# One rotary product per projection with its exchanged half from a VectorE shuffle, and new places for all operations of the layers and the closing block

## The chip, the core and the metric

The kernel runs on one core of one Trainium2 chip. The core has five engines that follow their own instruction lists: PE (TensorE, with its weight loads PEld), DVE (VectorE), ACT (ScalarE), POOL (GpSimd) and SP (SyncE, which issues the DMAs). They meet through semaphores alone. The metric is device time in microseconds (us), lower is better: the kernel before takes 2342.19 us, the median of three runs.

## The reference, cut to what matters

Four sequences of 512 rows of 128 channels go through a slot attention, a mixture of experts, six transformer layers and a quantised feed-forward block. The six layers are what the change touches:

```python
def _rope(x):                      # HD = 8, half = 4
    x1, x2 = (x[..., :half], x[..., half:])
    return concatenate([x1 * cos - x2 * sin, x1 * sin + x2 * cos], axis=-1)

for i in range(NL):                # NL = 6 layers, 16 heads of 8 channels
    xn = _adaln(x, noise_emb, n1_w[i], n1_b[i])
    q, k, v = split(xn @ qkv_w[i].T, 3)
    a = _attn(_rope(q), _rope(k), v, src_mask) @ so_w[i].T;  x = x + a
    xn = _adaln(x, noise_emb, n2_w[i], n2_b[i])
    q = _rope(xn @ cq_w[i].T);  k = _rope(context @ ck_w[i].T)
    a = _attn(q, k, context @ cv_w[i].T, ctx_mask) @ co_w[i].T;  x = x + a
    xn = _adaln(x, noise_emb, n3_w[i], n3_b[i])
    x = x + (gelu(xn @ f1_w[i].T + f1_b[i]) @ f2_w[i].T + f2_b[i])
```

## The kernel before, in words

Six layers times four sequences are 24 *visits*, `VISITS`. The four visits of a layer are independent of each other, and visit v needs the result of visit v - 4. The kernel runs them as a software pipeline that is written out by hand. Three tables of numbers, `OFFSETS`, `LAYER_OFFSETS` and `BLOCK_PLACES`, give every operation a place, with a step of `PERIOD` from visit to visit. `Places.moments` sorts the places of one engine, and each engine runs its operations in that sorted order. The numbers are nothing but sort keys: what an operation waits for is set by its semaphores, and an engine never runs ahead of an operation that waits.

One visit is this chain. `normalise_rows` (POOL) makes normal rows, `turn_rows` (PE, L1398) transposes them, `scale_shift` (ACT, L1598) applies the gain. `product` (PE, L1406) multiplies by the query and the key weights and, in the rotary step, by a second copy of each whose rows are exchanged by halves of a head (`qr`, `kr`, later `cqr`): so the two halves of a pair of PSUM banks hold the product and its exchanged product. `turn_products` (DVE, L1842) multiplies both by cosine and sine in one operation of 1024 columns, `rotate` (POOL, L1744) adds the halves. Then the sum is split into three bf16 parts: `first_part` (ACT, L1609), `less_first` (POOL, L1748), `second_part` (ACT, L1613), `third_part` (POOL, L1754). SP stores the parts to DRAM and loads them back in another layout (`store_queries`, `store_stage`, `load_queries`, `load_keys`).

The self attention of a visit takes 32 *max* steps (PE L1281 scores, DVE L1826 row maxima), in four groups, each followed by a split of the maxima (POOL L1757 to L1760), a transposition (PE L1348), a copy (ACT L1575) and two small DMAs. Then come 32 *exp* steps (PE L1292 shifted scores, ACT L1561 exponentials) and 16 products with the values (PE L1328). L1365 and L1372 transpose sums and rows, L1381 projects and L1871 (DVE) adds to the state. Cross attention is the same with L1315/L1833 (max), L1303/L1561 (exp) and L1340. The feed-forward part is L1438, L1634 and L1447. The `context` keys get the same rotary treatment once a layer, in two halves (L1414, L1849).

All scores, the rotary products and the feed-forward products take turns in a ring of three pairs of PSUM banks (`shared(..., 3)`): a PE step waits until the reader of the step that used its pair last is done. One further bank, `aux`, serves transpositions and projections one at a time. POOL and SP run their own lists in order, so a step that waits there holds all that stand behind it.

The closing block (four passes, b = 0 to 3, one per sequence; its DVE work at L1907 to L2013) starts for a sequence when the last layer's visit of that sequence is done, and so runs beside the visits 20 to 23.

Of the kernel before, what the change touches and what calls it, by code (L numbers as in the profile page):

```python
# [56 lines left out]
SECTION_GROUPS = {"next": ("n1", "q", "qr", "k", "kr", "v"), "self": ("so", "n2", "cq", "cqr"), "context": ("ck", "ckr", "cv"),  # L57
# [731 lines left out]
def store_key_part(sp, dst, parts, stage, stored):  # L789
# [5 lines left out]
VISITS = LAYERS * B  # L795
PER_UNIT = 2 * TB
# [4 lines left out]
N_HALF = B // 2 * N_CTX  # L801
# [5 lines left out]
PERIOD = 7152  # L807
OFFSETS = {
    "PE exp": (
        -54, 274, 479, 1118, 1587, 1668, 2002, 2177, 2281, 2529, 2558, 2737, 2915, 3047, 3271, 3428, 3673, 3908, 4042, 4177, 5174, 5350,  # L810
        5514, 5712, 5842, 5899, 6019, 6151, 6222, 6342, 6516, 6678),
    "ACT exp": (
        0, 328, 559, 1192, 1648, 1752, 2045, 2219, 2335, 2575, 2679, 2783, 3015, 3119, 3314, 3497, 3716, 3954, 4097, 4231, 5217, 5404,
        5568, 5755, 5896, 6000, 6104, 6208, 6312, 6416, 6558, 6720),
    "PE max": (
        -4071, -3915, -3695, -3574, -3537, -3301, -3267, -2938, -2712, -2313, -1955, -1933, -1769, -1604, -1474, -1276, -967, -20, 308,
        513, 677, 939, 1084, 1275, 1430, 1624, 1801, 1968, 2126, 2317, 2495, 2703),
    "DVE max": (
# [3 lines left out]
    "POOL split": (-2758, -1083, 1507, 3051),  # L822
    "PE turn maxima": (-2338, -201, 3104, 3394),
    "ACT copy maxima": (-1998, -123, 3217, 3439),
    "SP rows": (-1920, -45, 3295, 3517),
    "ACT copy": (4449, 6971),
    "PE gather": (4574, 7378),
    "DVE divide": (4642, 7446),
    "PE turn on": (7583,),
    "ACT copy on": (7651,),  # L830
    "PE project": (7921,),
    "DVE add": (8048,),
    "PE cross turn on": (16742,),
    "ACT cross copy on": (16820,),
    "PE cross project": (16900,),
    "DVE cross add": (17027,),
    "PE cross exp": (14938, 15050, 15181, 15221, 15457, 15615, 15811, 16139),
    "ACT cross exp": (15022, 15126, 15235, 15339, 15595, 15751, 15855, 16215),
    "PE cross max": (13529, 13642, 13691, 13803, 13868, 13950, 13990, 14128),
    "DVE cross max": (13564, 13688, 13768, 13850, 13930, 14010, 14090, 14170),  # L840
    "PE cross pv": (15291, 15479, 16007, 16333),
    "POOL cross split": (14270,),
    "PE cross turn maxima": (14407,),
    "ACT cross copy maxima": (14452,),
    "SP cross rows": (14530,),
    "ACT cross copy": (15693, 16450),
    "PE cross gather": (15834, 16528),
    "DVE cross divide": (15912, 16606),
    "DVE moments cross": (8407,),
    "DVE seed cross": (9124,),  # L850
    "POOL norm cross": (9212,),
    "PE turn cross": (10009,),
    "ACT scale cross": (10087,),
    "DVE moments ff": (17103,),
    "DVE seed ff": (17335,),
    "POOL norm ff": (17460,),
    "PE turn ff": (18000,),
    "ACT scale ff": (18118,),
    "DVE moments next": (-8255,),
    "DVE seed next": (-8135,),  # L860
    "POOL norm next": (-8047,),
# [145 lines left out]
def layers(nc, a, m, sem):  # L1007
# [88 lines left out]
    with nc.Block() as block:  # L1096
# [156 lines left out]
        def _(pe):  # L1253
# [147 lines left out]
            def product(kind, half, i):  # L1401
# [5 lines left out]
                if half:  # L1407
                    got.then_inc(x_ps[kind], 1)
# [888 lines left out]
```

## Time and profile before

| what | value |
|---|---|
| median of three runs | 2342.19 us (2342.07 to 2351.33) |
| the profiled execution | 2346.46 us |
| its span, first to last instruction | 2344.7 us |
| granted TensorE clock, mean | 0.904 |
| PE busy / weight loads busy | 1883.7 us (80%) / 798.6 us (34%) |
| DVE busy | 1655.5 us (71%) |
| ACT busy | 1483.1 us (63%) |
| POOL busy | 929.8 us (40%) |

A busy PE is the union of its matmuls' spans, whose ends are modelled and which overlap. The layers begin at about 424 us. From about 650 us to 1990 us every visit looks like the one before it; ahead of that the pipeline fills, and behind it the visits run out while the closing block runs.

### The profile page before, as it was taken

To read this page: it belongs to the slowest core of one execution; us is meant where nothing else is said; L and a number is where in the kernel's file an instruction comes from. 1 tells how busy PE (TensorE), PEld (TensorE's weight loads), DVE (VectorE), ACT (ScalarE), POOL (GpSimd) and SP (SyncE) were. 2 spreads that over 40 slices of the span, in tenths; PEclk is the share of its full clock that TensorE was granted. 3 is DMA by queue.
4 is the path that set the end of the run, shared out by engine and by line. 5 is a ranking of instruction groups with operands and counts; after the bars stand their busy time and mean duration, and the time that the engine had idled before them with its cause. 6 is when DMAs were issued, how large, how long until landed. Compare 5 with 4: busy or idle time off the path is not lost.

```text
span 2344.7 us, 36580 instructions
## 1 busy us (share of the span) xinstructions
PE 1883.7 (80%) x13318; PEld 798.6 (34%) x13318; DVE 1655.5 (71%) x3027; ACT 1483.1 (63%) x1840; POOL 929.8 (40%) x1420
## 2 busy tenths in 40 slices
PE   3564381167899999999999999999999999988651
PEld 2333271012233333333333333333334333333321
DVE  7766011367788887888878887888888887786456
ACT  2442020035678878878887877888877887767442
POOL 2443705123244453444444344444444445423421
PEclk9776696579999999999999999999999999989765
DMA  2001121322233433323433324432432333411100
GB/s 95 1 1 42 49 96 47 85 55 63 59 71 83 92 81 89 76 55 82 105 86 70 83 64 88 91 83 69 97 80 60 76 93 87 90 38 37 33 6 9
DMA packets 153713, 156.45 MB, mean 67 GB/s; under 512 B 32247, under 2 KB 137523, under 8 KB 153523
## 3 DMA queue, kind: packets, MB, share of 16 engines
q1 hardware_dynamic: 151487, 149.91, 27.1%
q0 software_dynamic: 2048, 4.20, 0.6%
q8 instruction: 107, 1.75, 0.3%
q14 instruction: 71, 0.58, 0.1%
HBM read 83.73 MB, written 67.85 MB: 65 GB/s over the span
## 4 chain that ended last, share of the span: by engine, by line
PE 58%; DVE 14%; ACT 4%; issue 4%; POOL 1%; DMA 1%; SPq 0%; POOLq 0%; DVEq 0%; ACTq 0%
PE ps L1328 14%; PE ps L1292 7%; DVE smax L1826 6%; PE ps L1281 6%; PE ps L1406 6%; PE ps L1447 4%; PE ps L1438 4%; PE ps L1340 4%; ACT big L1561 2%; PE ps L1381 2%; DVE rot L1842 2%; PE ps L1365 2%; PE ps L1303 1%; PE ps L1315 1%; PE ps L1398 1%
## 5 line engine op out<-in xcount | busy, mean ns | idle before, releaser
L1561 ACT ACTIVATE big<-ps 128x1024 f32<-128x1024 f32 x960 | 956.2, 1027 | 258.8 <-PE ps L1292 240.2
L1826 DVE TENSOR_REDUCE smax<-ps 128x2 f32<-128x1024 f32 x768 | 921.7, 1221 | 261.5 <-PE ps L1281 255.7
L1328 PE MATMUL ps<-big,vaug 128*32 128x512 f32 x3072 | 412.1, 615 | 2.9 <-ACT big L1561 2.9
L1281 PE MATMUL ps<-k,q 49*128 49x512 bf16 x1536 | 294.1, 391 | 64.3 <-DVE smax L1826 35.5
L1292 PE MATMUL ps<-q,k 52*128 52x512 bf16 x1536 | 295.4, 387 | 12.1 <-DVE smax L1826 5.6
L1757 POOL CAST mparts<-smax 128x16 bf16<-128x16 f32 x96 | 19.5, 203 | 569.1 <-DVE smax L1826 569.1
L1281 PEld LDWEIGHTS ps<-k,q 49*128 49x128 bf16 x1536 | 72.7, 94 | 310.5 <-DVE smax L1826 105.4
L1406 PE MATMUL ps<-xnT,w 128*128 128x512 f32 x288 | 166.8, 665 | 0.9 <-ACT xnT L1598 0.9
L1833 DVE TENSOR_REDUCE maxima<-ps 128x8 f32<-128x616 f32 x192 | 144.6, 795 | 31.6 <-PE ps L1315 30.0
L1292 PEld LDWEIGHTS ps<-q,k 52*128 52x128 bf16 x1536 | 75.2, 94 | 195.0 <-issue 90.2
L1748 POOL TENSOR_TENSOR hat<-rot,rparts 128x512 f32<-128x512 f32 x72 | 83.6, 1161 | 112.2 <-ACT rparts L1609 112.2
L1744 POOL TENSOR_TENSOR rot<-rot 128x512 f32<-128x512 f32 x72 | 91.5, 1271 | 74.2 <-DVE rot L1842 72.9
L1340 PE MATMUL ps<-big,vcaug 128*32 128x512 f32 x768 | 104.9, 617 | 14.3 <-ACT big L1561 6.5
L1754 POOL TENSOR_TENSOR rparts<-hat,rparts 128x512 bf16<-128x512 f32 x72 | 83.5, 1159 | 69.7 <-ACT rparts L1613 69.7
L1447 PE MATMUL ps<-w,hT 128*128 128x128 f32 x768 | 109.6, 287 | 1.6 <-ACT hT L1634 1.6
L1438 PE MATMUL ps<-xnT,w 128*128 128x512 f32 x192 | 108.6, 664 | 1.9 <-ACT xnT L1598 1.9
L1447 PEld LDWEIGHTS ps<-w,hT 128*128 128x128 f32 x768 | 92.5, 191 | 35.7 <-issue 32.5
L1842 DVE TENSOR_TENSOR rot<-ps,cs 128x1024 f32<-128x1024 f32 x72 | 87.7, 1218 | 22.8 <-PE ps L1406 21.9
L1328 PEld LDWEIGHTS ps<-big,vaug 128*32 128x32 f32 x3072 | 63.4, 109 | 116.1 <-issue 94.3
L1303 PE MATMUL ps<-cq,kc 52*128 52x512 bf16 x384 | 71.8, 394 | 11.4 <-DVE smax L1826 4.5
L1598 ACT ACTIVATE xnT<-ps,gain_next 128x512 f32<-128x512 f32 x24 | 18.5, 773 | 98.4 <-PE ps L1398 98.4
L311 PE MATMUL ps<-ident,hat 128*128 128x128 f32 x96 | 23.3, 389 | 68.0 <-DVE hat L126 48.1
(302 smaller groups left out, 2877.4 us busy)
## 6 DMA issues: line engine op xcount, KB each, us to landing
q<-scratch_queries SPq DMA_DIRECT2D x48, 384.0 KB, 5.6
k<-scratch_keys SPq DMA_DIRECT2D x48, 384.0 KB
cq<-scratch_cross_queries SPq DMA_DIRECT2D x48, 384.0 KB, 6.3
scratch_queries<-rparts SPq DMA_DIRECT2D x24, 384.0 KB, 2.4
scratch_keys<-rparts SPq DMA_DIRECT2D x24, 384.0 KB, 2.6
scratch_cross_queries<-rparts SPq DMA_DIRECT2D x24, 384.0 KB
scratch_queries<-rparts SPq DMA_DIRECT2D x24, 256.0 KB, 2.7
scratch_keys<-rparts SPq DMA_DIRECT2D x24, 256.0 KB, 2.8
```

What stands on the lines that cost most here:

```text
L1281: last = nc.tensor.matmul(out[:, u], m.q6[rows, v % 2, 2 * g + pr, qt * P:(qt + 1) * P], m.k6[rows, v % 2, 2 * g + pr, :], start=True, sto ...
L1292: last = nc.tensor.matmul(out[:, u], m.k6[rows, v % 2, 2 * g + pr, kt * P:(kt + 1) * P], m.q6[rows, v % 2, 2 * g + pr, :], start=True, sto ...
L1303: last = nc.tensor.matmul(out[:, u], m.kc6[rows, v % B, pair, :], m.cq[rows, pair, :], start=True, stop=True)
L1328: last = nc.tensor.matmul(m.ps[32 * j:32 * j + 32, pv_bank, :], of_head(m.vaug, v % 2 * TB + kt, g, j), of_quad("self", q)[:, j, :], start ...
L1340: last = nc.tensor.matmul(m.ps[32 * j:32 * j + 32, aux, :], of_head(m.vcaug, v % B, g, j), of_quad("cross", n)[:, j, :], start=(g % 2 == 0 ...
L1406: got = nc.tensor.matmul(banks(kind, i)[:, half, :], w_of(m, names[half]), m.xnT[:, xn[of_turn, i], :], start=True, stop=True)
L1438: nc.tensor.matmul(banks("up", 2 * v + c // 2)[:, c % 2], w_of(m, "f1")[:, c * P:(c + 1) * P], m.xnT[:, xn["ff", v], :], start=True, stop= ...
L1447: last = nc.tensor.matmul(m.ps[:, aux, t * P:(t + 1) * P], m.hT1[:, c, t * P:(t + 1) * P], w_of(m, "f2")[:, c * P:(c + 1) * P], start=(c = ...
L1561: nc.scalar.activation(of_quad(kind, p // 2)[:, p % 2 * 2:p % 2 * 2 + 2, :], banks("exp" if kind == "self" else "cross exp", p), ACT.Exp, ...
L1826: nc.vector.tensor_reduce(m.smax[:, n % 2, qt, :, pr], banks("max", i), AX.X, ALU.max).then_inc(s_read["self"], 1)
L1833: nc.vector.tensor_reduce(m.maxima[:, qt, :, PAIRS // 2 * half:PAIRS // 2 * (half + 1)], banks("cross max", i)[:, :, 0:PAIRS // 2 * N_CTX] ...
L1842: nc.vector.tensor_tensor(m.rot[:, rot[kind, i]], banks(kind, i), m.cs[:], ALU.mult).then_inc(x_read[kind], 1)
```

## The change

The weights of the exchanged copies (`qr`, `kr`, `cqr`, `ckr`) are gone from the weight table, and so is the second product. The product now fills one bank of its pair. DVE makes the exchanged half from it with `stream_shuffle` (it moves lanes within groups of 32; `OTHER_HALF` is lane XOR 4), and multiplies the product by the cosine, 512 columns each. POOL multiplies the exchanged half by the sine, and then adds as before. The context keys are made in one step of 308 columns where two halves stood.

```diff
+OTHER_HALF = [lane ^ (HD // 2) for lane in range(32)]
-PERIOD = 7152
+PERIOD = 6479
...
-            def product(kind, half, i):
...
-                got = nc.tensor.matmul(banks(kind, i)[:, half, :], w_of(m, names[half]), m.xnT[:, xn[of_turn, i], :], start=True, stop=True)
+            def product(kind, i):
+                name, of_turn = {"cross": ("cq", "cross"), "query": ("q", "next"), "key": ("k", "next")}[kind]
+                pe.wait_ge(t_xn[of_turn], i + 1)
+                out = free_banks(kind, i)
+                nc.tensor.matmul(out[:, 0, :], w_of(m, name), m.xnT[:, xn[of_turn, i], :], start=True, stop=True).then_inc(x_ps[kind], 1)
...
+            def context_products(n):
+                weights("context", n)
+                take_aux(x_read["context"], n + 1)
+                nc.tensor.matmul(m.ps[:, aux, 0:NC_ALL], w_of(m, "ck"), m.ctxT[:], start=True, stop=True).then_inc(x_ps["context"], 1)
...
             def rotate(kind, i):
-                pool.wait_ge(x_read[kind], 2 * (i + 1) if kind == "context" else i + 1)
+                pool.wait_ge(x_read[kind], i + 1)
                 x = turned(kind, i)
...
+                    r_chain.link(nc.gpsimd.tensor_tensor(x[:, 1, :], x[:, 1, :], m.cs[:, 1, :], ALU.mult))
                 nc.gpsimd.tensor_tensor(x[:, 0, :], x[:, 0, :], x[:, 1, :], ALU.add).then_inc(x_rot[kind], 1)
...
-                nc.vector.tensor_tensor(m.rot[:, rot[kind, i]], banks(kind, i), m.cs[:], ALU.mult).then_inc(x_read[kind], 1)
+                out, product = m.rot[:, rot[kind, i]], banks(kind, i)[:, 0, :]
+                nc.vector.stream_shuffle(out[:, 1, :], product, OTHER_HALF)
+                nc.vector.tensor_tensor(out[:, 0, :], product, m.cs[:, 0, :], ALU.mult).then_inc(x_read[kind], 1)
```

All numbers of the three tables are new as well, and so every engine's list stands in another order. Line numbers in the changed kernel differ by a few (L1281 is L1276, L1292 is L1287, L1328 is L1323, L1398 is L1393, L1406 is L1400, L1826 is L1819, L1833 is L1826, L2001 is L1996). Three places show what moved.

PE, in the middle of the layers, from the first transposition of the sums on (max scores read `k,q`, exp scores read `q,k`, products with the values read `big,vaug`). Before:

```order
L1365 MATMUL ps<-ident,xnT 128x128 x4
L1328 MATMUL ps<-big,vaug 32x512 x8
L1348 MATMUL ps<-ident_bf,mparts 12x128 x4
L1281 MATMUL ps<-k,q 128x512 x2
L1292 MATMUL ps<-q,k 128x512 x2
L1281 MATMUL ps<-k,q 128x512 x4
L1447 MATMUL ps<-w,hT 128x128 x4
```

The same place after:

```order
L1360 MATMUL ps<-ident,xnT 128x128 x4
L1323 MATMUL ps<-big,vaug 32x512 x4
L1276 MATMUL ps<-k,q 128x512 x2
L1323 MATMUL ps<-big,vaug 32x512 x4
L1343 MATMUL ps<-ident_bf,mparts 12x128 x4
L1276 MATMUL ps<-k,q 128x512 x4
L1287 MATMUL ps<-q,k 128x512 x2
L1323 MATMUL ps<-big,vaug 32x512 x4
L1287 MATMUL ps<-q,k 128x512 x2
L1436 MATMUL ps<-w,hT 128x128 x4
```

The two value products stood together; a max step now stands between them, and the two adjoining max steps are followed by an exp step and a value product.

PE, from the transposition of the next layer's rows (`ident,hat`) to its rotary products (`xnT,w`). Before:

```order
L1398 MATMUL ps<-ident,hat 128x128 x4
L1315 MATMUL ps<-kc,cq 128x77 x16
L1328 MATMUL ps<-big,vaug 32x512 x4
L1348 MATMUL ps<-ident_bf,mparts 12x128 x4
L1315 MATMUL ps<-kc,cq 128x77 x8
L1406 MATMUL ps<-xnT,w 128x512
L1292 MATMUL ps<-q,k 128x512 x2
L1281 MATMUL ps<-k,q 128x512 x2
L1406 MATMUL ps<-xnT,w 128x512
L1356 MATMUL ps<-ident_bf,mcparts 48x128 x4
L1406 MATMUL ps<-xnT,w 128x512
```

The same place after:

```order
L1393 MATMUL ps<-ident,hat 128x128 x4
L1287 MATMUL ps<-q,k 128x512 x2
L1276 MATMUL ps<-k,q 128x512 x2
L1323 MATMUL ps<-big,vaug 32x512 x4
L1351 MATMUL ps<-ident_bf,mcparts 48x128 x4
L1276 MATMUL ps<-k,q 128x512 x2
L1287 MATMUL ps<-q,k 128x512 x2
L1400 MATMUL ps<-xnT,w 128x512
L1360 MATMUL ps<-ident,xnT 128x128 x4
L1287 MATMUL ps<-q,k 128x512 x2
L1400 MATMUL ps<-xnT,w 128x512
```

Four rotary products (the fourth of before stands further down) are two now, and max and exp steps lead up to them where cross maxima did. The first of the two is now the key's; it was the query's.

DVE, in the last visit, from the add of visit 22's feed-forward part (`state,ps`) to the last visit's eight cross maxima (`maxima`); `vaug,vcaug` and `vaug,kc` are the closing block's scale and offset of pass 1. Before:

```order
L1871 TENSOR_TENSOR state<-state,ps 128x512
L1955 TENSOR_TENSOR x<-x,state 128x512
L1907 BN_STATS bn<-x 128x6 x4
L1910 BN_AGGR mv<-bn 128x2 x4
L2001 TENSOR_TENSOR vaug<-vaug,vcaug 128x2048
L2002 TENSOR_TENSOR vaug<-vaug,kc 128x2048
L1833 TENSOR_REDUCE maxima<-ps 128x2x4 x8
```

The same place after:

```order
L1866 TENSOR_TENSOR state<-state,ps 128x512
L1826 TENSOR_REDUCE maxima<-ps 128x2x4 x2
L1989 SCALAR_TENSOR_TENSOR shift<-mv,rstd 128x4
L1826 TENSOR_REDUCE maxima<-ps 128x2x4 x5
L2008 SCALAR_TENSOR_TENSOR x<-ps,step,x 128x128 x4
L1950 TENSOR_TENSOR x<-x,state 128x512
L1902 BN_STATS bn<-x 128x6 x4
L1905 BN_AGGR mv<-bn 128x2 x4
L1996 TENSOR_TENSOR vaug<-vaug,vcaug 128x2048
L1997 TENSOR_TENSOR vaug<-vaug,kc 128x2048
```

The block's work stood ahead of the last visit's cross maxima; it stands behind them now (one of the eight even stands ahead of the add).

## Rows read from the trace of the kernel before

**Rows 1.** The page, part 2: 40 slices of 58.6 us, in tenths.

```profile
PE   3564381167899999999999999999999999988651
PEclk9776696579999999999999999999999999989765
```

**Rows 2.** Busy time by stretch: start:end, length, busy us of each engine, clock, DMA.

```profile
1020.00:1080.00 60.00, 58.02 (x460) 22.32 (x460) 50.23 (x74) 48.67 (x58) 25.82 (x42) 1.00 0.36 80
...
2220.00:2280.00 60.00, 30.88 (x194) 14.54 (x192) 38.39 (x88) 22.40 (x25) 18.78 (x20) 0.60 0.05 10
```

**Rows 3.** Chain that ended last, in order of time: start us, us, what.

```profile
672.15 2.09 PE ps L1438 x4
...
1987.66 2.09 PE ps L1438 x4
...
2274.51 5.63 PE ps L1438 x8
```

**Rows 4.** Groups by line and shape: xcount | busy us, mean ns | idle before.

```profile
L1826 DVE TENSOR_REDUCE smax<-ps 128x2 f32<-128x1024 f32 x768 | 921.7, 1221 | 261.5 <-PE ps L1281 255.7
...
L1406 PE MATMUL ps<-xnT,w 128*128 128x512 f32 x288 | 166.8, 665 | 0.9 <-ACT xnT L1598 0.9
...
L1744 POOL TENSOR_TENSOR rot<-rot 128x512 f32<-128x512 f32 x72 | 91.5, 1271 | 74.2 <-DVE rot L1842 72.9
L1842 DVE TENSOR_TENSOR rot<-ps,cs 128x1024 f32<-128x1024 f32 x72 | 87.7, 1218 | 22.8 <-PE ps L1406 21.9
...
L725 DVE COPY state<-ps 128x512 f32<-128x512 f32 x8 | 5.5, 692 | 69.1 <-PE ps L611 69.1
```

**Rows 5.** Timeline of PE, one visit: start us, us, what [idle before].

```profile
1039.97 0.66 PE L1398 MATMUL ps<-ident,hat 128*128 128x128 f32 x4
...
1042.71 1.12 PE L1406 MATMUL ps<-xnT,w 128*128 128x512 f32 x2
1043.76 0.39 PE L1292 MATMUL ps<-q,k 52*128 52x512 bf16 x2
1043.99 0.38 PE L1281 MATMUL ps<-k,q 49*128 49x512 bf16 x2
...
1074.02 0.38 PE L1281 MATMUL ps<-k,q 49*128 49x512 bf16 x2
```

**Rows 6.** Timeline of PE where two max steps adjoin.

```profile
1025.13 0.39 PE L1281 MATMUL ps<-k,q 49*128 49x512 bf16 x2 [0.89 <-DVE smax L1826]
```

**Rows 7.** Timeline of DVE at the same place.

```profile
1023.84 4.62 DVE L1826 TENSOR_REDUCE smax<-ps 128x2 f32<-128x1024 f32 x4 [1.57 <-PE ps L1281]
```

**Rows 8.** Waits from 741 to 1985 us: us in total, times, longest.

```profile
POOL mparts L1757 <- DVE smax L1826: 397.1, 72, 12.8
...
PE ps L1281 <- DVE smax L1826: 16.9, 23, 0.9
```

**Rows 9.** Timeline of POOL behind a query's rotary product.

```profile
1046.85 1.27 POOL L1744 TENSOR_TENSOR rot<-rot 128x512 f32<-128x512 f32 x1 [1.84 <-DVE rot L1842]
1049.22 1.16 POOL L1748 TENSOR_TENSOR hat<-rot,rparts 128x512 f32<-128x512 f32 x1 [1.11 <-ACT rparts L1609]
```

**Rows 10.** The page, part 6, DMA issues: xcount, KB each, us to landing.

```profile
q<-scratch_queries SPq DMA_DIRECT2D x48, 384.0 KB, 5.6
...
scratch_queries<-rparts SPq DMA_DIRECT2D x24, 256.0 KB, 2.7
```

**Rows 11.** Chain that ended last, first visit, 423 to 470 us.

```profile
436.54 3.80 PE ps L1406 x4
...
465.05 0.62 PE ps L1281 x2
```

**Rows 12.** Timeline of DVE in the last visit.

```profile
2223.34 2.26 DVE L2001 TENSOR_TENSOR vaug<-vaug,vcaug 128x2048 f32<-128x2048 f32 x1
...
2227.96 5.74 DVE L1833 TENSOR_REDUCE maxima<-ps 128x8 f32<-128x616 f32 x8
```

**Rows 13.** Timeline of PE at the same place.

```profile
2228.81 0.44 PE L1315 MATMUL ps<-kc,cq 49*128 49x77 bf16 x8 [5.07 <-DVE maxima L1833]
```

More of the change, by code:

```diff
@@ L904 @@
 }
 LAYER_OFFSETS = {
-    "SP weights self": 3444,
-    "PE gain cross": 4409,
-    "DVE gain cross": 4454,
-    "SP weights out": 9898,
-    "SP weights ff": 13087,
-    "PE gain ff": 13687,
-    "DVE gain ff": 13732,
-    "SP weights next": -10224,
-    "PE gain next": -8352,
-    "DVE gain next": -8307,
-    "PE context values": 13224,
-    "ACT copy context values": 13334,
-    "SP load context": 9598,
-    "SP weights context": 4883,
-    "PE product context 0": 6383,
-    "DVE rope context 0": 6468,
@@ L922 @@
-    "PE product context 1": 7733,
-    "DVE rope context 1": 7818,
-    "POOL rotate context": 7913,
-    "ACT first context": 8073,
-    "POOL less context": 8173,
-    "ACT second context": 8313,
-    "POOL third context": 8413,
-    "SP store context": 8553,
+    "SP weights self": 4290,
+    "SP weights context": -9223,
+    "SP weights out": 12083,
+    "SP weights ff": 12427,
+    "SP weights next": -8418,
+    "PE gain cross": 4623,
+    "DVE gain cross": 4780,
+    "PE gain ff": 13253,
@@ L930 @@
+    "DVE gain ff": 13422,
+    "PE gain next": -6099,
+    "DVE gain next": -6054,
+    "PE context values": 12520,
+    "ACT copy context values": 12986,
+    "SP load context": 10800,
+    "PE product context": 7881,
+    "DVE rope context": 7917,
+    "POOL rotate context": 8654,
+    "ACT first context": 8795,
+    "POOL less context": 9050,
+    "ACT second context": 9194,
+    "POOL third context": 9749,
+    "SP store context": 9830,
 }
 BLOCK_PLACES = {
-    "SP block rows": (159673, 166825),
@@ new lines @@
+    "DVE block begin": (148551, 155250, 162909, 168146),
+    "POOL block root first": (150112, 155853, 163062, 168755),
+    "DVE block first": (150271, 157068, 163652, 170690),
+    "POOL block root second": (150543, 157124, 163793, 171225),
+    "DVE block second": (151261, 157179, 164054, 172645),
+    "POOL block scale": (151935, 158154, 164325, 173306),
+    "POOL block bias": (160957, 161018, 171106, 205999),
+    "DVE block quantise": (152277, 159023, 164765, 177407),
+    "ACT block round": (152639, 159055, 164766, 178279),
@@ L967 @@
+    "DVE block output": (162585, 165765, 177279, 237711),
+    "SP block store": (171530, 197200, 213333, 241498),
 }
@@ L2070, in _ @@
                         turn_products(kind, i)
-                for half in range(2):
-                    for n in due(f"DVE rope context {half}", now):
-                        turn_context(half, n)
+                for n in due("DVE rope context", now):
+                    turn_context(n)
 def build(nc, a):
```

285 lines of the change are left out of this document (128 added, 157 removed), and 10 rows, old and new, of the table OFFSETS.

## The prediction

> **What bounds the kernel now.** I read the page's slices first: PE is at 9 tenths from the 12th slice to the 35th, and its clock is at 9 tenths or more there, which is the full level, 2.4 GHz [rows 1]. Only the filling and the tail are loose. The stretches say the same with numbers: in 60 us of the middle PE is busy for 58.0, DVE for 50.2, ACT for 48.7 and POOL for 25.8 [rows 2]. One visit takes (1987.66 - 672.15) / 19 = 69.2 us, from the first feed-forward product of visit 0 to that of visit 19 [rows 3]. So the execution falls into 247 us of filling (from 424), 19 periods of 69.2 us, and 359 us of tail. Scaled to a period, PE is busy for 66.9 us and idle for 2.3; DVE works 58 us and ACT 56.
>
> A busy PE could be one whose matmuls merely overlap, so I looked at where calls start. A rotary product starts at 1042.71 and the next call at 1043.76; an exp step starts 0.23 us ahead of the max step behind it [rows 5]. These distances return unchanged wherever nothing waits: PE issues one call behind the other. Its idle time is waiting for score readers, above all where two max steps adjoin: DVE sat idle for 1.57 us, then got four row maxima at once, and PE waited 0.89 us for it [rows 6, 7]. That kind cost 16.9 us in 18 visits [rows 8].
>
> The Trainium skill (Perfetto Trace Analysis, Identifying the Most-Contended Engine) says that matmul busy time is not a good measure of how close TensorE is to its limit, and that the busy share of LDWEIGHTS is a better one. PEld is busy for 22.3 of 60 us here, 37% [rows 2]; by that rule PE has room, and what it saves would be lost in other waits. By the start distances the saving counts in full; by the rule the steady part would give nothing, and the time would be that of the third rival below.
>
> **The change part by part.** *Products.* 72 of the 144 rotary products go, three per visit, at 1.05 us from start to start [rows 5]; the trace lists each as two passes of 665 ns, 288 in all, which overlap [rows 4]. That is 3 x 1.05 = 3.2 us of PE per visit, and since PE is what every visit fills, all of it lies on the path. The context's single step of 308 columns instead of four of 154 saves some 0.6 us a layer by the same rate, 0.15 us a visit. PE's busy 66.9 us become 63.6.
>
> *DVE.* One product of 1024 columns at 1.22 us becomes a shuffle and a product of 512 columns each [rows 4]. A shuffle is nowhere in the trace. The nearest row is a copy of 512 columns from PSUM, 0.69 us, which I take as the lower end, since a shuffle reads and writes the same columns and does more with them; the upper end is a pass at half that speed, as long as the row maxima over 1024 columns, 1.22 us [rows 4]. I take 0.69, the row with the same columns and memories. Then a rotary step is 1.38 instead of 1.22 us, 0.5 us more per visit (at the upper end 2.1 us more). DVE then works 58.5 of some 65 us, 90%: still under PE, but with less room than its present 84%.
>
> *POOL.* Three more operations on 128x512 per visit at 1.27 us [rows 4] are 3.8 us. POOL works 25.8 of 60 us [rows 2] and mostly waits for row maxima (397 us in 18 visits [rows 8]), so its time costs nothing. But each sits in a chain that splits and stores the rotated rows, and key and query follow each other in POOL's list: the query's sum waits for the key's product and sum, 2.5 us, before its own 2.5 us.
>
> *Places.* The idle 2.3 us per visit is the order's. Where PE now issues two value products and then a max, an exp and two max steps, the new order puts a max step between the value products, so that DVE begins one value product earlier, and puts an exp step and a value product behind the adjoining max steps. I expect 0.7 of the 0.94 us (16.9 / 18) of this kind to go, none of the rest: 1.6 us of idle time. The steady period becomes 63.6 + 1.6 = 65.2 us, 4.0 us less.
>
> *The chain behind it.* From the transposition of the next rows at 1039.97 to the first max step of that visit at 1074.02 are 34.0 us [rows 5]. In the new order the calls that stand between the two, each with the distance to its successor that it has in the trace, make 27.6 us (32.6 in the old one). That stretch must hold the whole rotary chain. Worked out with rows: 3.0 us of PE to the key's product, 1.1 for it, 1.4 DVE; then POOL one behind the other: 4 x 1.27 for two products and two sums, 4 x 1.16 for the subtractions, 8 gaps of 0.07 [rows 9], together 10.3; 16 us so far, and 17 with a wait for ACT. Three stores are issued in 1.3 and land after 2.7 us, and a load lands after 5.6, the second of a pair a little later [rows 10]: 26.5 to 28.5 us in all. So the chain just fits, with a wait of up to 1 us that falls together with others in the same stretch. I count nothing for it, and carry 1.5 us in the range.
>
> *Filling.* The first visit's rotary products run at half clock: four take 3.8 us up to the first DVE step and more behind it, and the first max starts at 465.05 [rows 11]. Two products fewer are some 3.5 us less of PE there, two POOL products at 1.27 us more; the loads of the keys no longer wait behind those of the queries. With some PE work saved on the way to visit 0's feed-forward part, 8 us less (range 0 to 15).
>
> *Tail.* In the last visit the block's scale and offset, 2.3 us each, stand on DVE ahead of the cross maxima, and PE waits 5.07 us for the first of these [rows 12, 13]. The new order has the maxima first: 5 us. Other block work moves both ways, some of it ahead of rotary steps of visit 22; the rotary part of visits 20 to 23 saves 3 us of PE at most, since PE is busy half of the time there (30.9 of 60 us, at 0.60 of the full clock [rows 2]). I take 12 us less, between 30 less and 10 more.
>
> *Sum.* 19 x 4.0 = 77 in the steady part, 8 in the filling, 12 in the tail: 97 us off the profiled execution's 2346.5, thus 2249. That execution lies 4.3 us above the median of the runs, 2342.2; off the median it is 2245 us.
>
> **The rivals** (all against the median, 2342). *More waiting.* DVE at 90% leaves fewer gaps, and the chain above may need 29 us. If idle time rises to 4 us the period is 67.6: 19 x 1.6 = 30 us, and with 4 and 5 us for filling and tail the time is 2303. For it speaks that both margins shrink at once; against it that DVE is fed more evenly.
>
> *Less waiting.* If nearly all reader waits go (0.5 us left), the period is 64.1: 97 us, and with 10 and 25 us at the ends 2210.
>
> *PE is not the bound.* If what the products free is lost in waits for DVE and ACT, which work 84% and 81% of the period, the period stays at 69.2 and only the ends gain some 7 us: 2335. For it speaks that waits for readers are already what PE's idle time is made of; against it that neither reader is full and that PE's calls stand start to start.
>
> *The chain sets the period (slower).* If the stretch from the transposition to the first max keeps its present 34.0 us because its loads and its waits on ACT do not shrink, and POOL's two added products come on top, it takes 36.5 us where the order holds 27.6. The period is then 65.2 + 36.5 - 27.6 = 74.1, and 19 x 4.9 = 93 us more give 2423 after 12 less at the ends. It turns into a loss from a stretch of 31.6 us on, where the period is 69.2 again. Against it: the old chain has long idle pieces in it, since the old order places the key late; its parts add up to less than 28.5.
>
> **How the numbers follow.** Main case 0.60, with 1.0 to 3.0 us of idle time and the ranges of the ends 2245 +- 30; more waiting 0.18; less waiting 0.15; PE not the bound 0.03; chain-bound 0.04. The range from 2205 to 2300 leaves out the last two, half of the upper rival and some of the lower one, together just under 2 in 10. About 0.5%, 12 us, is what a measurement can tell from no change. Faster by more than that: 0.60 + 0.15 + 0.18 = 0.93; the third rival and the crossing of the fourth make 0.04 for the same; slower 0.03.
>
> **What would show it.** A profile of the changed kernel should have 144 passes at the rotary product's line, 72 shuffles near 0.7 us, and 19 periods of about 65 us with PE busy for 97% or more. The wait of PE for row maxima behind adjoining max steps should be mostly gone, and the last visit's cross maxima should no longer make PE wait for 5 us. I am wrong if shuffles take over 1.2 us, if max steps wait for loads of queries or keys in every visit (the chain), or if PE's busy share falls while the period stays.

## The result, and the profile after

The changed kernel takes 2237.53 us, the median of four runs (2235.99 to 2239.56), against 2346.76 us for the kernel before on the same chip: a ratio of 0.9535, with a 95% interval from 0.9507 to 0.9563. The forecast was 2245 us, in a range from 2205 to 2300. The profiled execution has a span of 2235.3 us; that of before had 2344.7 us.

The total came out close to the forecast, but not by the forecast's parts. The first rows are from the chain of work that ended last, in order of time (start us, us, what), at the first feed-forward product of visit 0 and of visit 19; they answer to [rows 3].

```profile
652.88 1.91 PE ps L1427 x4
...
1913.43 1.91 PE ps L1427 x4
```

A visit takes (1913.43 - 652.88) / 19 = 66.34 us, where it took 69.24. The same product seen on TensorE's own timeline starts at 649.8 in visit 0 (670.5 before) and at 1910.3 in visit 19 (1986.0 before). With these two moments the 109.4 us between the spans divide so:

| part | forecast | measured |
|---|---|---|
| filling, to visit 0's feed-forward product | -8 | -20.7 |
| 19 steady visits | -77 | -55.0 |
| tail, from visit 19's feed-forward product | -12 | -33.7 |

The next two rows are the busy time in one stretch of the steady part, of the kernel before and of the changed kernel (start:end, length, busy us of PE, PEld, DVE, ACT and POOL, clock, DMA share, GB/s).

```profile
741.00:1880.00 1139.00, 1106.31 (x8366) 435.59 (x8367) 926.73 (x1315) 918.19 (x1115) 492.25 (x801) 1.00 0.35 80
```

```profile
741.00:1880.00 1139.00, 1088.80 (x8556) 427.79 (x8556) 966.33 (x1482) 953.38 (x1162) 582.24 (x893) 1.00 0.37 82
```

Scaled to a visit, PE was busy for 67.2 us and idle for 2.0; now it is busy for 63.4 and idle for 2.9. The work fell by 3.8 us, and 0.9 us of that came back as waiting. Where it waits is in the list of PE's waits of the changed kernel, over the same stretch (us in total, times, longest):

```profile
PE ps L1276 <- DMA q<-scratch_queries: 18.7, 17, 1.9
PE ps L1298 <- ACT big L1549: 7.3, 18, 0.4
...
PE ps L1287 <- DVE smax L1819: 0.6, 2, 0.3
```

The wait for row maxima of [rows 8], 0.94 us per visit, has gone from the list but for small pieces. In its place every one of 17 visits waits for the load of its queries, 18.7 / 17 = 1.1 us. This is the chain for which the prediction counted nothing. Behind two of the three longest of these waits (1.94 and 1.71 us) TensorE's granted clock falls to half, 1.2 GHz, for a moment. Those two visits take 67.5 and 68.8 us, where the others at the same place of their layers take 65.3 and 66.6. The first of them, on PE's timeline and as a stretch of busy times (the clock is the third number from the end):

```profile
771.64 0.39 PE L1276 MATMUL ps<-k,q 49*128 49x512 bf16 x2 [1.94 <-DMA q<-scratch_queries]
```

```profile
773.40:776.80 3.40, 3.40 (x17) 0.95 (x10) 2.54 (x6) 2.11 (x3) 2.88 (x5) 0.50 0.02 5
```

Without these two visits the period is 66.1 us (here and below the mean over the four places of a layer).

The groups by line and shape (xcount | busy, mean ns of one | idle before) show the rotary's pieces beside [rows 4]:

```profile
L1736 POOL TENSOR_TENSOR rot<-rot,cs 128x512 f32<-128x512 f32 x72 | 91.9, 1277 | 101.0 <-DVE rot L1837 101.0
L1737 POOL TENSOR_TENSOR rot<-rot 128x512 f32<-128x512 f32 x72 | 91.3, 1268 | 5.6
L1400 PE MATMUL ps<-xnT,w 128*128 128x512 f32 x144 | 82.6, 657 | 1.7 <-ACT xnT L1586 1.7
L1836 DVE STREAM_SHUFFLE rot<-ps 128x512 f32<-128x512 f32 x72 | 52.6, 731 | 0.0
L1837 DVE TENSOR_TENSOR rot<-ps,cs 128x512 f32<-128x512 f32 x72 | 48.5, 673 | 0.0
```

The 288 passes of products are 144, and a shuffle takes 0.73 us.

Now the chain itself, in one visit. First PE's timeline (start us, us, what, idle before): the transposition of the next rows, the key's product, and the first max of that visit, with its wait. Then SyncE's, the issue of the DMAs.

```profile
1271.84 0.66 PE L1393 MATMUL ps<-ident,hat 128*128 128x128 f32 x4
...
1275.05 1.12 PE L1400 MATMUL ps<-xnT,w 128*128 128x512 f32 x2
...
1301.72 0.39 PE L1276 MATMUL ps<-k,q 49*128 49x512 bf16 x2 [1.12 <-DMA q<-scratch_queries]
```

```profile
1288.08 0.34 SPq L784 DMA_DIRECT2D scratch_queries<-rparts  x1
1288.45 0.43 SPq L785 DMA_DIRECT2D scratch_queries<-rparts  x1
1288.93 0.49 SPq L786 DMA_DIRECT2D scratch_queries<-rparts  x1
1289.52 1.15 SPq L1160 DMA_DIRECT2D k<-scratch_keys  x2
1290.71 1.36 SPq L1146 DMA_DIRECT2D k<-scratch_neg_mask  x2
1292.11 1.01 SPq L1151 DMA_DIRECT2D q<-scratch_queries  x2
```

From the transposition to the first max are 29.9 us. Up to the stores, 16.2 us, the estimate of 16 to 17 held to the step. The end did not: the queries' loads are issued behind the keys' and the masks', and the first max comes 9.6 us after the first of them is issued, as soon as the second has landed. The page's DMA issues give 8.1 us to landing where [rows 10] had 5.6:

```profile
q<-scratch_queries SPq DMA_DIRECT2D x48, 384.0 KB, 8.1
```

In the kernel before the keys' loads were issued some 8 us behind the queries'; now they are issued 2.4 us ahead of them.

### The profile page after: what moved, and what is told of

Its sections match the earlier page's. It is cut to its first block, busy times and chain, and to the rows that moved or that the text cites. A ratio compares the mean times of both kernels' runs of the same rounds, so it can differ in the third digit from the quotient of the medians.

```text
span 2235.3 us, 36409 instructions
## 1 busy us (share of the span) xinstructions
PE 1791.6 (80%) x13134; PEld 765.2 (34%) x13138; DVE 1653.7 (74%) x3177; ACT 1476.8 (66%) x1840; POOL 1021.2 (46%) x1498
## 4 chain that ended last, share of the span: by engine, by line
PE 39%; DVE 11%; DMA 9%; ACT 7%; POOL 7%; issue 6%; SPq 2%; DVEq 0%; POOLq 0%; ACTq 0%
PE ps L1323 9%; DMA q<-scratch_queries 9%; PE ps L1287 5%; PE ps L1436 5%; PE ps L1276 4%; DVE smax L1819 4%; ACT big L1549 4%; POOL hat L126 3%; PE ps L1427 3%; PE ps L1335 2%; PE ps L1400 2%; PE ps L1310 2%; PE ps L1298 1%; DVE maxima L1826 1%; PE ps L1376 1%
## 5 line engine op out<-in xcount | busy, mean ns | idle before, releaser
L1819 DVE TENSOR_REDUCE smax<-ps 128x2 f32<-128x1024 f32 x768 | 921.5, 1219 | 204.4 <-PE ps L1276 181.2
L1323 PE MATMUL ps<-big,vaug 128*32 128x512 f32 x3072 | 419.8, 617 | 0.0
L1276 PE MATMUL ps<-k,q 49*128 49x512 bf16 x1536 | 298.1, 391 | 68.3 <-DMA q<-scratch_queries 51.5
L1287 PE MATMUL ps<-q,k 52*128 52x512 bf16 x1536 | 300.6, 390 | 16.1 <-DVE smax L1819 8.3
L1826 DVE TENSOR_REDUCE maxima<-ps 128x8 f32<-128x616 f32 x192 | 150.1, 795 | 42.8 <-PE ps L1310 40.5
L1276 PEld LDWEIGHTS ps<-k,q 49*128 49x128 bf16 x1536 | 72.8, 94 | 297.6 <-ACT big L1549 99.3
L1718 POOL TENSOR_SCALAR var_next<-mv_next 128x4 f32<-128x4 f32 x24 | 5.6, 233 | 356.1 <-DVE mv_next L1886 356.1
L1287 PEld LDWEIGHTS ps<-q,k 52*128 52x128 bf16 x1536 | 75.7, 94 | 187.2 <-DVE smax L1819 63.9
L1736 POOL TENSOR_TENSOR rot<-rot,cs 128x512 f32<-128x512 f32 x72 | 91.9, 1277 | 101.0 <-DVE rot L1837 101.0
L1427 PE MATMUL ps<-xnT,w 128*128 128x512 f32 x192 | 101.4, 635 | 4.6 <-ACT xnT L1586 1.8
L1323 PEld LDWEIGHTS ps<-big,vaug 128*32 128x32 f32 x3072 | 62.6, 109 | 99.9 <-issue 96.9
L1400 PE MATMUL ps<-xnT,w 128*128 128x512 f32 x144 | 82.6, 657 | 1.7 <-ACT xnT L1586 1.7
L1563 ACT COPY mt<-ps 12x512 bf16<-12x512 bf16 x96 | 54.0, 563 | 37.0 <-PE ps L1343 36.9
```

Of the source, the lines that this page charges most:

```text
L1276: last = nc.tensor.matmul(out[:, u], m.q6[rows, v % 2, 2 * g + pr, qt * P:(qt + 1) * P], m.k6[rows, v % 2, 2 * g + pr, :], start=True, sto ...
L1287: last = nc.tensor.matmul(out[:, u], m.k6[rows, v % 2, 2 * g + pr, kt * P:(kt + 1) * P], m.q6[rows, v % 2, 2 * g + pr, :], start=True, sto ...
L1323: last = nc.tensor.matmul(m.ps[32 * j:32 * j + 32, pv_bank, :], of_head(m.vaug, v % 2 * TB + kt, g, j), of_quad("self", q)[:, j, :], start ...
L1400: nc.tensor.matmul(out[:, 0, :], w_of(m, name), m.xnT[:, xn[of_turn, i], :], start=True, stop=True).then_inc(x_ps[kind], 1)
L1427: nc.tensor.matmul(banks("up", 2 * v + c // 2)[:, c % 2], w_of(m, "f1")[:, c * P:(c + 1) * P], m.xnT[:, xn["ff", v], :], start=True, stop= ...
L1736: r_chain.link(nc.gpsimd.tensor_tensor(x[:, 1, :], x[:, 1, :], m.cs[:, 1, :], ALU.mult))
```

## The experiments

Each ran beside the kernel before on the same chip. "Per visit" is read as above, from visit 0's feed-forward product to visit 19's, and "tail" from there to the end, both in us of the one profiled execution. The diffs are cut to the lines that matter.

| kernel | median us | ratio to before (95%) | per visit | tail |
|---|---|---|---|---|
| changed kernel | 2237.53 | 0.9535 (0.9507 to 0.9563) | 66.34 | 325 |
| new places, old rotary | 2291.13 | 0.9752 (0.9717 to 0.9788) | 68.96 | 328 |
| old places, new rotary | 2387.04 | 1.0165 (1.0130 to 1.0201) | 70.70 | 360 |
| old places, new rotary, ScalarE later | 2389.50 | 1.0181 (1.0156 to 1.0205) | 70.91 | 359 |
| old places, new rotary, products kept | 2397.05 | 1.0206 (1.0189 to 1.0223) | 71.12 | 362 |
| extra product inside the stretch | 2241.50 | 0.9551 (0.9517 to 0.9586) | 66.51 | 326 |
| extra product outside it | 2251.23 | 0.9587 (0.9552 to 0.9621) | 67.32 | 327 |
| extra max of the cross product | 2253.94 | 0.9595 (0.9572 to 0.9619) | 66.63 | 324 |
| extra max of the query product | 2241.43 | 0.9539 (0.9515 to 0.9563) | 66.29 | 326 |
| masks early | 2234.68 | 0.9509 (0.9485 to 0.9533) | 66.05 | 327 |
| masks early, query stores staged | 2219.05 | 0.9453 (0.9426 to 0.9481) | 65.47 | 321 |
| query's sine on VectorE | 2255.64 | 0.9616 (0.9590 to 0.9643) | 67.06 | 323 |
| staged stores and sine | 2236.70 | 0.9529 (0.9506 to 0.9552) | 66.49 | 322 |

### Which half of the change did it

**New places, old rotary.** The code of the kernel before with the new table; of each pair of products the second stands right behind the first:

```diff
-    "PE product query": (-5508,),
+    "PE product query 0": (-5508,),
+    "PE product query 1": (-5507,),
```

> The kernel before (two products per rotary kind, one multiplication of both halves on VectorE, one addition on GpSimd) with the changed kernel's places; each second product stands right behind the first. My theory (matmul work plus a wait of about 1.1 us per visit for the queries' load, 66.3 us per visit in the changed kernel): TensorE gets 3.2 us per visit back, while the chain to the queries' load loses one GpSimd pass per kind, so its wait goes: 66.3 - 1.1 + 3.2 = 68.4 us per visit, 2237 + 24 x 2.1 = about 2288 us (2275 to 2305). Rival, the new places make the whole gain: 2235 to 2245. Rival, the removed products make the whole gain: 2335 to 2345.

The time, 2291 us, is what was expected, though a step of it was not: the wait for the queries' load stayed (19.8 us in 16 visits), and the products added 2.6 us per visit. The load's 8.3 us to landing come with the new places, then: with the old places and the new rotary, the next run, it is 5.6 us as before. No run moves the keys' loads alone, so that it is they that lengthen it is likely, but not shown by itself.

**Old places, new rotary.** The code of the changed kernel with the old table; the one product stands where the second stood.

```diff
-    "PE product query 0": (-7307,),
-    "PE product query 1": (-7150,),
+    "PE product query": (-7150,),
```

> The changed kernel's rotary (one product, shuffle, two GpSimd passes) in the order of the kernel before; each product stands at the place of the former second product. My theory: TensorE does 3.2 us less per visit, but the chains are longer by one GpSimd pass of 1.27 us per kind and the order around them is the old one, so part of it turns into waiting: 67 to 69 us per visit, about 2295 us (2270 to 2335). Rival, the removed products make the whole gain by themselves: 2235 to 2250. Rival, the new places make the whole gain: 2340 or above.

It missed upward: 2387 us, 1.65% slower than the kernel before, with three products of 1.05 us less for TensorE to do in every visit. So the new rotary alone is a loss, and the new places alone win 58 us by the medians. Only in the new places does the new rotary win as well: 2.6 us per visit between the first run and the changed kernel. PE's waits in the old places, from 741 to 1985 us:

```profile
PE ps L1417 <- ACT big L1539: 17.7, 18, 1.1
PE ps L1266 <- DVE smax L1809: 16.7, 22, 0.9
PE ps L1350 <- ACT mct L1559: 13.7, 18, 0.8
PE ps L1266 <- ACT big L1539: 12.7, 16, 2.4
PE ps L1390 <- DVE maxima L1816: 9.9, 18, 0.6
```

Of these five only the second was there before [rows 8]; the other four are 54 us in 18 visits, 3.0 us per visit. The third is the easiest to follow. Here is PE's timeline at that place, before and in this run:

```profile
1391.52 0.40 PE L1356 MATMUL ps<-ident_bf,mcparts 128*48 128x128 bf16 x4
1391.86 1.12 PE L1406 MATMUL ps<-xnT,w 128*128 128x512 f32 x2
1392.82 0.38 PE L1365 MATMUL ps<-ident,xnT 128*128 128x128 f32 x2
```

```profile
1410.10 0.40 PE L1341 MATMUL ps<-ident_bf,mcparts 128*48 128x128 bf16 x4 [0.19 <-POOL mcparts L1743]
1411.26 0.63 PE L1350 MATMUL ps<-ident,xnT 128*128 128x128 f32 x4 [0.76 <-ACT mct L1559]
```

The transposed cross maxima must be copied by ScalarE before the bank that both transpositions use is free. Before, a rotary product lay between the two and covered the copy. It was removed, and PE now stands still for 0.76 us.

The fourth is for the most part no wait of every visit. Once a layer ScalarE waits 2.7 us for GpSimd's rotary of the context keys, which it did not in the kernel before; PE then waits 2.3 us for an exponential's bank, and during that wait or just behind it the granted clock falls to half, 1.2 GHz. ScalarE's waits, PE's timeline in one of these visits, and the stretch behind it:

```profile
ACT cond_rows L1587 <- POOL rot_c L1727: 10.9, 4, 2.7
```

```profile
1422.65 0.39 PE L1266 MATMUL ps<-k,q 49*128 49x512 bf16 x2 [2.35 <-ACT big L1539]
```

```profile
1424.50:1427.90 3.40, 3.40 (x19) 0.41 (x12) 1.81 (x5) 3.10 (x4) 1.70 (x4) 0.50 0.56 157
```

The five visits with this stop take 74.1 us on average, where these visits took 70.5 in the kernel before; the other 14 take 69.5 against 68.8. So 18 of the 28 us that the steady part loses against the kernel before are lost in five visits.

**Is it GpSimd's longer rotary, through ScalarE's queue?** In that run ScalarE waited 35.8 us in 18 visits for GpSimd's second rotary pass. This run moves ScalarE's roundings behind the next exponentials:

```diff
-    "ACT first query": (-6726,),
+    "ACT first query": (-6586,),
```

> The run with the old places and the new rotary (2387 us, 70.7 us per visit), with one thing changed: ScalarE's first and second roundings of each kind stand 140 of the table's units later in ScalarE's own order, one or two exponentials further back; the other engines keep their order word for word. In that run ScalarE stood in its queue 2.0 us per visit for GpSimd's second rotary pass, and TensorE waited 3 us per visit for ScalarE. My theory (the added GpSimd pass stops ScalarE in its queue, and the exponentials behind it hold TensorE's banks): most of these 3 us go, 68.5 to 69.5 us per visit, about 2345 us (2320 to 2360). Rival, another part of the old order does it: 2375 to 2395 us.

The theory fell. ScalarE's wait for the rotary passes of queries and keys has left its list, and the time is the same. In the 14 visits without the context's stop the move gave 0.3 us (69.1 against 69.5), not the 1.2 to 2.2 us that were expected. PE's waits for the rest changed places: the one at the feed-forward products went, the one of the max steps for an exponential's bank grew from 12.7 to 22.3 us (half of that growth in the stop, which is 3.6 us long here), and the copy of the cross maxima still costs this:

```profile
PE ps L1350 <- ACT mct L1559: 13.7, 18, 0.8
```

**Or is it the cover that was removed?** Old places and new rotary, but three products that nobody reads stand where the first products stood:

```diff
+                if spare:
+                    nc.tensor.matmul(out[:, 1, :], w_of(m, name), m.xnT[:, xn[of_turn, i], :], start=True, stop=True)
+                    return
```

> Old places and new rotary, as in the run of 2387 us, with three products per visit given back to TensorE at the places where the first products of the kernel before stood; nothing reads them, they only take 3.2 us of TensorE per visit. Theory after the run with ScalarE moved (2389.5 us): in the old order the removed products had covered latencies (a max read by VectorE, the copy of the cross maxima, a bank held by an exponential), and the uncovered waits took their place, so giving the products back costs little: 0 to +0.8 us per visit, 2385 to 2407 us. The rest above the kernel before (2349 us) is then the price of the longer GpSimd chains in that order. Rival, the removal did bring its 3.2 us in the old order as well, and the new rotary's GpSimd and VectorE passes cost more than 100 us there: 2387 + 24 x 3.15 = 2463 us (2445 to 2465).

As the theory had it: 3.2 us more of TensorE per visit cost 0.4 us per visit, 10 us in all (0.6 us in the visits without the context's stop, nothing in those with it). The waits for the cross maxima (9.9 us) and for their copy (13.7 us) are gone from PE's list. In the old order the products took little time, because waits stood ready in their place. From the kernel before to this run the period grows by 1.9 us; that is what the shuffle, GpSimd's three passes and the new treatment of the context cost there. The growth is 3.6 us in the five visits with the context's stop and 1.3 us in the others; which step carries the 1.3 us is open.

### Does the chain to the queries' load count?

**An extra product inside the stretch**, ahead of the cross projection, and **one outside it**, ahead of the cross query's product:

```diff
+                if kind == "cross":
+                    nc.tensor.matmul(m.ps[:, aux, :], w_of(m, "co"), m.on[:], start=True, stop=True)
```

> The changed kernel with one more 128x512 f32 product per visit (1.05 us of TensorE, its result is overwritten), ahead of the cross projection, which stands between the transposition of the next visit's rows and that visit's first max, where TensorE now waits about 1.1 us per visit for the queries' load. My theory (the wait is what the chain is longer than the work in between): the product fills the wait, +0 to +0.3 us per visit, 2237 to 2245 us. Rival, TensorE's work alone sets the period: +1.05 us per visit, 2262 us. Rival, a loop of latencies sets the period and TensorE's amount of work doesn't: 2237 us.

```diff
+                if kind == "cross":
+                    nc.tensor.matmul(out[:, 1, :], w_of(m, name), m.xnT[:, xn[of_turn, i], :], start=True, stop=True)
```

> The changed kernel with the same extra product, now ahead of the cross query product, outside the stretch between that transposition and the first max. My theory: nothing there waits, so the whole product counts, +1.05 us x 24 = 25 us, about 2262 us (2255 to 2268). Rival, TensorE's work alone: 2262 us too. Rival, a loop of latencies sets the period: 2237 to 2242 us. Together with the run inside the stretch it tells the three apart.

PE's wait for the queries' load, inside and then outside:

```profile
PE ps L1276 <- DMA q<-scratch_queries: 7.8, 10, 1.4
```

```profile
PE ps L1276 <- DMA q<-scratch_queries: 21.2, 16, 2.9
```

Inside, 1.05 us of work raised the period by 0.17 us and shrank the wait from 18.7 to 7.8 us. Outside, it raised the period by 0.98 us and the wait stayed. A part of this difference is the clock. In the profiled execution of the outer product the granted clock falls to half (1.2 GHz) in three of the 19 visits, each time behind a wait for the load of 2.2 to 2.9 us, and these visits take 2.6 to 3.3 us more than the others at their places; with the inner product it never falls. Over the visits at full clock the period is 66.1 us in the changed kernel, 66.5 with the inner product and 66.9 with the outer one: of 1.05 us, 0.4 are paid inside and 0.75 outside. The medians show 4 and 14 us, where the full price is 25. The profiled execution of the outer product fits its forecast (2262.64 us), but its other runs go down to 2244 us, and its median misses the forecast. So the outer product costs some two to four times what the inner one does, which TensorE's amount of work alone does not explain; nor does a loop of latencies without TensorE, since the outer product counted.

**Shorten the chain at its end.** The masks' DMAs go ahead of the stores; in the second run each part of the queries is stored as soon as it is rounded, too.

```diff
+    "SP load masks": (-5300,),
```

> The changed kernel with the two mask DMAs of each visit issued on SyncE some 14 us earlier, so that the queries' loads no longer stand behind them (2 issues of 0.67 us). The last store of the queries lands 0.4 us before their load is issued in the changed kernel (1291.71 against 1292.11), so at most 0.4 us of the wait goes. My theory (the chain to the queries' load sets 1.1 us per visit): -0.4 us x 22 = -9 us, about 2229 us (2222 to 2237). Rival, TensorE's work alone sets the period and the wait is incidental: 2237 us.

```diff
-    "SP store query": (-4331,),
+    "SP store query 0": (-4700,),
+    "SP store query 1": (-4480,),
+    "SP store query 2": (-4331,),
```

> As the run with the early masks, and the three stores of the queries' parts are issued one by one, each when its part is there, as those of the keys are. Then only the store of all three parts follows the last GpSimd step, and it lands about 1.2 us earlier (1290.5 against 1291.71). My theory: queries are loaded 1.6 us earlier per visit, more than the wait of 1.1 us, so the wait goes whole: 66.3 - 1.1 = 65.2 us per visit, 2237 - 25 = about 2212 us (2205 to 2222). Rival, TensorE's work alone: 2237 us. Rival, the transfers of keys and queries share the DMA engines, and the earlier issue only makes the transfer longer: 2230 to 2237 us.

Masks early give 0.3 us per visit, of the 0.4 expected, but that is the clock, which does not fall in this run: at full clock the period is 66.1 us in both kernels. Against the changed kernel the intervals overlap, so no gain of the masks is shown. With staged stores the period is 65.47 us and the time 2219.05 us, 5.5% under the kernel before and clear of the changed kernel's interval. PE's wait for the load and, from the page, the load itself:

```profile
PE ps L1286 <- DMA q<-scratch_queries: 3.3, 5, 1.0
```

```profile
q<-scratch_queries SPq DMA_DIRECT2D x48, 384.0 KB, 8.7
```

The wait shrinks from 1.1 to 0.2 us per visit, and the period by 0.87 us, of which 0.2 us is the clock, which does not fall here either. The rival of the shared DMA engines has a small part of the truth, since the load that is issued earlier takes 8.7 us, not 8.1. This is the best version of the study.

### What do VectorE's and GpSimd's passes cost?

One more pass of VectorE, a maximum of 0.68 us that is not used, over the cross product (outside the stretch) or over the query product (inside):

```diff
+                if kind == "cross":
+                    nc.vector.tensor_reduce(m.extra[:, i:i + 1], product, AX.X, ALU.max)
```

> The changed kernel with one more pass of VectorE over the cross query product per visit (a maximum over 128x512 in PSUM, about 0.65 us; its result isn't used), ahead of the multiplication, outside the chain to the queries' load. My theory (VectorE's amount of work doesn't count, only its place): 0 to +0.3 us per visit, 2237 to 2245 us. Rival, VectorE is the bound: +0.65 us x 24 = 16 us, 2253 us.

> The same extra pass of VectorE, now over the query product, inside the chain to the queries' load. My theory: the chain gets longer by the whole pass, and nothing hides it: +0.65 us x 23 = 15 us, about 2252 us (2246 to 2256). Rival, the chain doesn't count: 2237 to 2242 us. Rival, VectorE is the bound: 2253 us here and with the pass over the cross product as well.

Both forecasts were wrong, and in opposite ways. Outside, the pass costs 0.29 us per visit in the profile and some 15 us, 0.6 per visit, by the medians. It keeps the product's bank, and PE has new waits for it and for the row maxima behind it:

```profile
PE ps L1287 <- DVE rot L1839: 7.9, 17, 0.5
...
PE ps L1287 <- DVE smax L1819: 6.1, 17, 0.4
```

Inside, next to nothing is lost: the period stays, and the median is 4 us higher. GpSimd does the key's two passes first and comes to the query 0.7 us after VectorE has finished it, so 0.68 us more on VectorE does not lengthen the chain; PE's lateness behind VectorE fills the wait for the load (11.3 us left of 18.7). GpSimd's timeline in the changed kernel shows it: the query's pass starts where the key's ends, while VectorE's last step for the query ended at 1279.47. With the extra pass it still starts there.

```profile
1277.59 1.27 POOL L1736 TENSOR_TENSOR rot<-rot,cs 128x512 f32<-128x512 f32 x1 [3.69 <-DVE rot L1837]
1278.94 1.27 POOL L1737 TENSOR_TENSOR rot<-rot 128x512 f32<-128x512 f32 x1
1280.16 1.29 POOL L1736 TENSOR_TENSOR rot<-rot,cs 128x512 f32<-128x512 f32 x1
```

So it goes as with the products: what lies inside the stretch is mostly paid out of the wait, what lies outside mostly in time. A bound by VectorE's amount of work is ruled out, since the same pass costs 4 us at one place and some 15 at the other.

**Give the query's sine back to VectorE**, alone and with the staged stores:

```diff
+                    nc.vector.tensor_tensor(out[:, 1, :], out[:, 1, :], m.cs[:, 1, :], ALU.mult).then_inc(x_sine, 1)
```

> The changed kernel with the multiplication by the sine of the query kind alone given back from GpSimd (1.27 us) to VectorE, in a pass of its own behind the one that frees the product's bank. My theory: the chain to the queries' load runs through GpSimd's queue, so 1.27 us less there takes the wait of 1.1 us away as the staged stores did: 65.3 to 65.6 us per visit, 2213 to 2222 us. Rival, GpSimd's pass is hidden beside other steps of the chain (the extra pass of VectorE over the query product cost 4 us only): 2234 to 2242 us.

> Early masks, staged query stores and the query's sine on VectorE together. With the staged stores 0.2 us of the wait for the queries' load is left per visit, so my theory is that nothing more is to be had: 2212 to 2222 us, as with the staged stores alone (2219 us). Rival, the chain to the queries' load still hides behind other waits and its further 1.27 us count: 2195 to 2205 us.

The first lost against the changed kernel, the second against the staged stores. VectorE's pass took 1.36 us, not the 0.67 of the pass with one input in PSUM:

```profile
L1845 DVE TENSOR_TENSOR rot<-rot,cs 128x512 f32<-128x512 f32 x24 | 32.5, 1356 | 0.0
```

The row maxima behind it came late, the cross scores waited for their banks, and in one visit ScalarE's rounding of the query came 1.84 us late for GpSimd, where that wait is 0.43 us in the changed kernel. Without the staged stores 13.2 us of waiting for the load in 15 visits are left, and PE has a new wait:

```profile
PE ps L1299 <- DVE smax L1822: 14.3, 34, 0.7
```

## Why the prediction was right, and where it was not

- **The products.** 3.35 us less PE work per visit, with the context, was forecast; 3.8 us were measured. That they count nearly in full (2.6 us per visit from the first run to the changed kernel) holds for the new order only. In the old one they gave 0.4 us: there the mechanism of the third rival was the right one, and what the products freed was lost in waits for ScalarE and VectorE. The prediction read full counting off the start distances; the test with the kept products shows that an engine whose calls stand start to start can still be covering other waits, each of which comes up when its cover goes.
- **The places.** The wait for row maxima went as said. But the idle time, 1.6 us by the forecast, is 2.9, and PE is busy for 95.6% of the steady part, not 97 or more. The step that failed is "So the chain just fits", with "I count nothing for it". The prediction's own sign of being wrong, max steps that wait for loads in every visit, came true. The mis-sized term is the queries' load: 5.6 us and a little, from [rows 10], became 9.6 us from issue to first max, with the keys' loads right in front of it. The price of a transfer was taken from a row in which it ran without that neighbour. Nor did the wait fall together with others in the stretch: in the visit shown these others, 0.9 us, stand beside its 1.12 us. Taking most of the wait away (staged stores) brings the period to 65.47 us; 65.2 was forecast.
- **The rivals.** The steady part lies between the main case and "More waiting": the period is 66.34 us, where they had 65.2 and 67.6, and the idle time 2.9 us, where they had 1.6 and 4. The chain is that rival's, 29 us by its terms and 29.9 measured. That the total still ended near the forecast is due to the ends.
- **Filling and tail.** Both ranges were too small (0 to 15 less, 30 less to 10 more; 20.7 and 33.7 less were measured). With the new places alone 13.4 of the first and 30.6 of the second are there already. The last visit's cross maxima no longer stop PE for the 5.07 us of [rows 13], as said, but the larger part lies ahead of them: visit 19's feed-forward product to that point took 237 us and takes 212. From visit 19 on the feed-forward products of successive visits stood 74, 74, 78 and 63 us apart; they stand 71, 65, 63 and 57 apart in the changed kernel, and 72, 65, 64 and 57 with the new places and the old rotary. So it is the new order of the last visits and of the block beside them. The forecast took the block's other moves as a draw. Which of the moves made the gain was not tried.
- **VectorE and GpSimd.** The shuffle is 0.73 us, near its lower end. Whether GpSimd's "time costs nothing" is not settled: its passes are in the chain to the queries' load, and the one attempt to take one out put a longer pass on VectorE in its place. In the old order GpSimd's rotary of the context did cost time, in five visits.
- **The last term.** The 4.3 us by which the profiled execution lay above the median were a difference between executions: with a fourth run the median of the kernel before is 2346.76 us, level with that execution. By these medians the gain is 109 us, and 97 were forecast.

The errors were 22 us in the steady part one way and 34 at the ends the other. They cancelled to 12 us of the gain, and the last term brought the forecast to within 8 us of the median. That closeness is luck, and the total is no proof of its parts.

## What to carry to other kernels

When work is taken off the engine that bounds a kernel, look up what stood behind each removed call: it may have covered a copy or a bank that is now waited for, and then the order has to be made anew before anything is won. When an order is changed, price each load by what will be in flight beside it, not by its present row. And where an engine waits for a chain in every visit, work between the chain's start and its end is cheap as long as the wait lasts; the same work elsewhere cost two to four times as much here. Before two profiled executions are compared by their periods, compare their granted clocks visit by visit.

## What the runs showed of the hardware

VectorE's pass over two inputs in SBUF met GpSimd's pass over SBUF in the run with the query's sine on VectorE. In 22 of 24 visits it began some 0.44 us after GpSimd's pass, ran 0.55 us past that pass's end, and took 1.37 to 1.38 us. In the first visit it began 0.20 us after that pass, took 1.61 us, and ended 0.55 us past it again. In one visit both began together: then VectorE needed 0.68 us, and GpSimd's two passes took 3.06 us where two take 2.54. VectorE's timeline in an ordinary visit and in that one, then GpSimd's in the same two:

```profile
1153.29 1.38 DVE L1845 TENSOR_TENSOR rot<-rot,cs 128x512 f32<-128x512 f32 x1
```

```profile
490.18 0.68 DVE L1845 TENSOR_TENSOR rot<-rot,cs 128x512 f32<-128x512 f32 x1
```

```profile
1152.85 1.27 POOL L1740 TENSOR_TENSOR rot<-rot 128x512 f32<-128x512 f32 x1
```

```profile
490.18 3.06 POOL L1740 TENSOR_TENSOR rot<-rot 128x512 f32<-128x512 f32 x2
```

So VectorE's pass ended 0.55 us behind GpSimd's however late it began, and where it ended first, GpSimd's passes took 0.52 us more: one waits for the other, for all but 0.13 to 0.16 us of a pass of 0.68. The Trainium skill (SBUF — State Buffer, Who interferes with whom) says that a VectorE instruction with two SBUF inputs contends with a GpSimd instruction that reads SBUF, that the port pair they share is an exclusive lock for which the order of issue decides, and that with at most one SBUF input, outside the 2-port modes, VectorE does not contend. This trace agrees: the sine's pass waits, and the cosine's pass, with its other input in PSUM, takes 0.67 us in the 47 cases with a GpSimd pass beside it as in the 25 without. Which of the two was issued first in the visit with the common start, the trace does not tell.
